# Graph attention and relational message passing: VectorE masks scores ahead of query and output-weight remainders, and half of the last pair's first value row goes in front of the first scores

## The reference, cut to what matters

```python
y = cond_layer_norm(x, cond, ...)
q = (y @ wq + bq).reshape(N, 4, 128) * 128 ** -0.5
k = (y @ wk + bk).reshape(N, 4, 128)
v = (y @ wv + bv).reshape(N, 4, 128)
scores = einsum('ehd,ehd->eh', q[src], k[dst])         # one for each edge and head
attn = softmax of scores over the edges of one source node
x = x + segment_sum(attn * v[dst], src) @ wo + bo
y = cond_layer_norm(x, cond, ...)
x = x + relu(y @ m_w1 + m_b1) @ m_w2 + m_b2
```

## Time and profile before

| | |
|---|---|
| median of three runs | 2318.28 us |
| profiled execution | 2313.26 us |
| its span | 2311.5 us |
| TensorE matmul busy | 2195.7 us, 95% |
| VectorE busy | 1577.9 us, 68% |
| ScalarE busy | 1121.3 us, 49% |
| GpSimd busy | 533.8 us, 23% |

### The profile page before, as it was taken

One profiled execution on the slowest core, in us unless ns is written; L12 is line 12 of the kernel. 1 busy time (PEld: TensorE's weight loads), 2 busy tenths in 40 slices (PEclk: granted clock), 3 DMA queues, 4 the chain that ended last, 5 costly groups with the idle time before them and its releaser, 6 DMA issues.

```text
span 2311.5 us, 36692 instructions
## 1 busy us (share of the span) xinstructions
PE 2195.7 (95%) x13898; PEld 1903.4 (82%) x13898; DVE 1577.9 (68%) x3347; ACT 1121.3 (49%) x1808; POOL 533.8 (23%) x399
## 2 busy tenths in 40 slices
PE   3899979999999999999999999999999999999998
PEld 1565678899888889988888998888899888877877
DVE  9999985588775468877547788754778774343233
ACT  6166643577633357763336775333777533231321
POOL 4000000366400046630005662000665200000000
PEclk9999989999999999999999999999999999999999
DMA  9997781210131020031002103111110421062044
GB/s 250 298 282 243 233 272 35 56 34 23 51 110 31 20 66 23 23 96 68 29 23 63 34 12 109 64 29 31 45 45 1 136 74 29 1 127 37 1 71 106
DMA packets 137379, 189.59 MB, mean 82 GB/s; under 512 B 61285, under 2 KB 61733, under 8 KB 137211
## 3 DMA queue, kind: packets, MB, share of 16 engines
q1 hardware_dynamic: 133208, 180.48, 28.1%
q10 hardware_dynamic: 4003, 6.79, 1.0%
HBM read 155.16 MB, written 32.07 MB: 81 GB/s over the span
## 4 chain that ended last, share of the span: by engine, by line
PE 76%; DVE 12%; ACT 5%; issue 5%; DVEq 1%; DMA 1%; SPq 1%; POOL 0%; ACTq 0%
PE PS L1038 10%; PE PS L1066 9%; PE PS L943 6%; PE PS L945 6%; PE PS L944 6%; PE PS L1052 6%; PE PS L929 5%; PE PS L933 4%; PE PS L930 4%; PE PS L1194 4%; PE PS L1204 4%; PE PS L850 4%; PE PS L801 2%; ACT prob L1435 1%; PE PS L862 1%
## 5 line engine op out<-in xcount | busy, mean ns | idle before, releaser
L782 POOL TENSOR_SCALAR prob<-prob,inv_den 125x1000 f32<-125x1000 f32 x160 | 444.4, 2777 | 0.0
L770 POOL TENSOR_TENSOR rstd<-var_eps,neg_half 125x2 f32<-125x2 f32 x45 | 35.5, 788 | 953.4 <-DVE var_eps L1598 953.4
L1435 ACT ACTIVATE prob<-prob,neg_max 125x1254 f32<-125x1254 f32 x160 | 215.6, 1347 | 56.7 <-DVE neg_max L1950 56.6
L1945 DVE CUSTOM_DVE_ANT_0 prob<-PS,sbias 125x1254 f32<-125x1254 f32 x160 | 233.1, 1457 | 10.0 <-issue 7.3
L1066 PE MATMUL PS<-pT_hi,v_hi 125*128 125x250 f32 x800 | 236.2, 295 | 0.0
L1964 DVE TENSOR_TENSOR pT_lo<-PS,pT_hi 125x1000 fp32r<-125x1000 f32 x160 | 191.1, 1194 | 50.7 <-ACT pT_hi L1452 50.7
L1066 PE MATMUL PS<-pT_lo,v_hi 125*128 125x250 f32 x800 | 224.2, 280 | 0.0
L1066 PE MATMUL PS<-pT_hi,v_lo 125*128 125x250 f32 x800 | 222.6, 278 | 0.0
L1052 PE MATMUL PS<-ident,prob 125*125 125x125 f32 x1600 | 201.1, 273 | 5.6 <-DVE pT_lo L1967 5.5
L1052 PEld LDWEIGHTS PS<-ident,prob 125*125 125x125 f32 x1600 | 195.6, 188 | 12.5 <-issue 7.6
L1450 ACT ACTIVATE pT_hi<-PS 125x1000 fp32r<-125x1000 f32 x160 | 161.9, 1012 | 81.3 <-PE PS L1052 81.3
(11 more groups left out here) (335 smaller groups left out, 5585.6 us busy)
## 6 DMA issues: line engine op xcount, KB each, us to landing
basis_t<-in_L_gnn_basis_dram SPq DMA_DIRECT2D x320, 192.0 KB, 4.9
sbias<-score_bias SPq DMA_DIRECT2D x40, 548.6 KB
adj<-adj SPq DMA_DIRECT2D x20, 546.9 KB
w_lo_raw<-in_L_gnn_m_w_dram SPq DMA_DIRECT2D x8, 1024.0 KB, 6.5
score_bias<-biases SPq DMA_DIRECT2D x10, 548.6 KB
adj<-count SPq DMA_DIRECT2D x10, 546.9 KB
xc<-x_lat SPq DMA_DIRECT2D x12, 448.0 KB
x_first<-x_lat SPq DMA_DIRECT2D x10, 448.0 KB
```

Source lines behind the costliest of these rows:

```text
L782: pool.tensor_scalar(prob[u % 3][:, 0:SPLIT], prob[u % 3][:, 0:SPLIT], inv_den[0:T, u % 4:u % 4 + 1], None, ALU.mult)\
L1435: act.activation(prob[u % 3][:], prob[u % 3][:], ACT.Exp, bias=neg_max[0:T, u % 4:u % 4 + 1], accum_out=den[0:T, u % 4:u % 4 + 1]).then_in ...
L1945: v.tensor_tensor_reduce(prob[u % 3][:].rearrange("p (j s) -> p j s", j=3), PS[0:T, 0:3, 0:SB], sbias[p % 2][a][:].rearrange("p (j s) -> p ...
```

## The change

VectorE's order in attention: for a = 1, q_low(i+1) comes directly behind masking(i, 1); before it stood at the end of a = 0, ahead of masking(i, 1). The first three quarters of the output weights' remainder come in heads 17, 18 and 19, for a = 0, behind pT_low and ahead of the inverse; before they stood at the end of heads 16, 17 and 18. The last quarter comes after head 19 in both. TensorE's order: of the value row (4, 0), 6 matmuls go ahead of scores(0, 0), the 7 others stay behind it. Nothing is added to or taken from what is computed.

```diff
-            def rows(bank, a, x_hi, x_lo, w_hi, w_lo, row3, before=None):
+            def rows(bank, a, x_hi, x_lo, w_hi, w_lo, row3, before=None, chunks=range(4)):
 
                 o = PS[0:T, bank, :]
                 n = slice(T * a, T * (a + 1))
-                for k in range(4):
+                for k in chunks:
                     if before:
                         before(k)
                     pe.matmul(o, x_hi[:, k, n], w_hi[:, k, :], start=(k == 0), stop=False)
...
+                def last_value_rows(a, chunks, row3):
+                    p = NP - 1
+                    return rows(qkv_bank(v_lo_done, 2 * p + a), a, yT_hi[p % 2], yT_lo[p % 2], wv_hi, wv_lo,
+                                row3, chunks=chunks)
+
                 for i in range(4 * NP):
                     for a in range(2):
+                        if i == a == 0:
+                            qkv_bank_free(pe, v_lo_done, 2 * (NP - 1), lay)
+                            last_value_rows(0, (0, 1), None)
                         scores(i, a)
-                        if i == 0:
+                        if i == 0 and a == 0:
+                            last_value_rows(0, (2, 3), bv3).then_inc(v_ps.sem, 1)
+                        elif i == 0:
                             value_rows(NP - 1, a)
                         if i >= 1:
                             turn(i - 1, a)
...
+                def wo_low(k):
+                    wait(v, w_hi_done, lay, k)
+                    v.tensor_tensor(wo_lo[:, k, :], wo_raw[:, k, :], wo_hi[:, k, :].bitcast(fp32),
+                                    ALU.subtract).then_inc(w_lo_done.sem, 1)
+
                 for i in range(4 * NP):
                     for a in range(2):
                         masking(i, a)
+                        if a == 1 and 2 <= i + 1 < 4 * NP:
+                            q_low(i + 1)
                         if i == 0:
                             value_low(NP - 1, a)
                         if i >= 1:
                             pT_low(i - 1, a)
+                        if a == 0 and i > 4 * NP - 4:
+                            wo_low(i - (4 * NP - 4) - 1)
                         inverse(i, a)
-                        if a == 0 and 2 <= i + 1 < 4 * NP:
-                            q_low(i + 1)
-                    if i >= 4 * NP - 4:
-                        k = i - (4 * NP - 4)
-                        wait(v, w_hi_done, lay, k)
-                        v.tensor_tensor(wo_lo[:, k, :], wo_raw[:, k, :], wo_hi[:, k, :].bitcast(fp32),
-                                        ALU.subtract).then_inc(w_lo_done.sem, 1)
+                wo_low(3)
```

## The result

The changed kernel took 2281.0 us, the median of four runs (2279.12 to 2284.91); the kernel before took 2317.93 beside it (four runs, 2311.95 to 2318.28). The ratio is 0.9849, with a 95% interval of 0.9828 to 0.987: faster by 1.5%, some 36 us. The execution profiled took 2284.91 us, its span is 2283.2 us, against 2313.26 and 2311.5 before. Behind TensorE's part the lines stand ten lower, so masking is L1955 (L1945 before), q_low L1879, the inverse L1966 and L1968, pT_low L1974 and L1977, and wo_low has a line of its own, L1982.

A forecast was written before the change was run, and what follows sets the result against it. TensorE was taken as the bound, with its idle time to be won. Terms 1.10 + 0.66 + 2.85 + 2.81 + 0.97 = 8.39 us a layer, 33.6 for four, gave 2279.7 or 2284.6; 2282 was taken, 80% range 2274 to 2297.

The forecast's parts named there:

- The value row: Handover into attention: six value matmuls ahead of the first scores let the second scores come earlier, 1.10 us a layer.
- Both bounds: Value row: 1.40 us of matmuls just fits ahead of the first scores; an open accumulation costs -0.1 to +0.1, taken as 0.
- The head from 1 to 2: Head 1: q_low behind masking lets head 2's first scores start at about 840.72 instead of 841.38, 0.66 us.
- its two bounds: Length of q_low in its new place: between 0.37 and 0.73 us.
- The repeating heads: 15 heads from head 2 to 17: the wait on masking and q_low goes, 0.19 us each, 2.85 us a layer.
- The floor of 9.15: Shortest repeating head if TensorE never stops: 4.56 plus 4.60 us, about 9.15 against the measured 9.334.
- Heads 17 and 18: wo_low behind pT_low lets masking start with its scores; heads fall from 10.65 to 9.20 and 9.29 us, gain 2.81.
- head 19: Last head: second scores come 4.65 us after the first instead of 5.55, carrying 0.97 us into the layer's end.
- The slower rival: q_low is held until GpSimd's normalisation ends, making heads 9.72 us and the kernel 2327 us; chance 0.05.
- q_low as the last release: q_low replaces masking as TensorE's last release, so the repeating heads gain nothing: 2296 us on the median's scale; chance 0.15.
- The margin: Repeating head: q_low releases TensorE 0.15 to 0.2 us before TensorE is ready for the next scores.
- The profile's scale: The profiled execution's 2313.3 us less 33.6 gives 2279.7; the same share off the median gives 2284.6.

The follow-up runs named there:

- e8_nine_ahead: The changed kernel with nine of the 13 value matmuls ahead of the first scores instead of six: 2280.48 us, ratio 0.9854 to the kernel before.
- e1_value: The kernel before with half of the value row ahead of the first scores as the only edit: 2317.82 us, ratio 1.0001.
- e7_before_q_twice: The kernel before with each q_low from head 2 on computed twice in its old place: 2351.97 us, ratio 1.015.
- e5_q_twice: The changed kernel with each q_low from head 2 on computed twice: 2282.83 us, ratio 0.9851 to the kernel before.
- e11_value_filled: The kernel before with the value row edit alone, plus nine unread matmuls in TensorE's wait before head 2's first scores: 2310.5 us, ratio 0.9977.
- e3_outw: The kernel before with the three output-weight remainders moved behind pT_low as the only edit: 2310.93 us, ratio 0.9983.
- e9_q_behind_pT: The changed kernel with q_low one place later, behind pT_low: 2418.84 us, ratio 1.0438 to the kernel before.
- e6_q_thrice: The changed kernel with each q_low from head 2 on computed three times: 2317.48 us, ratio 1.0006 to the kernel before.
- e10_tail: The changed kernel with the last two output-weight quarters' remainders in head 19 and the output bias split earlier: 2279.16 us, ratio 0.9844 to the kernel before.

## Why the prediction was right

It said 2282 us, 2274 to 2297, faster with 0.92; it is 2281.0. What decided is that idle time was read off start-to-start distances and not off wait lists: one of the two largest terms, 2.60 of 8.51 us a layer, was one that no list names. That the total is only 1 us off is in part luck: 2282 was put between 2279.7 on the profile's scale and 2284.6 on the median's, the attention stages gave 34.3 us and the medians differ by 36.9. By its own steps:

- **The value row, 1.10 us a layer.** 1.15. Both bounds held: the cover was just long enough (the first scores 1.95 after the last query columns in both), and an accumulation left open cost nothing seen. `e8_nine_ahead` shows the edge of the cover. What the step missed is the company: alone the edit gives nothing (`e1_value`), and nothing in the prediction said so. Its sum went by terms that were taken as independent, and they were so only because the query edit was in it too.
- **The head from 1 to 2, 0.66.** 1.04. The order of events was right, the size of q_low was not: the prediction took the upper of its two bounds, 0.73, and it took 0.41. The transposes of that head then wait for pT_low (0.15 in the record, at 833.96; they start 0.89 us after the last three scores, where 0.57 is usual). That makes head 2 0.31 us longer than before, so of the 1.04 only 0.73 is left one head later, near the 0.66. The wait did not go, it moved by a head; the prediction asked for scores only.
- **The repeating heads, 15 x 0.19 = 2.85.** 14 x 0.186 = 2.60, for head 2 does not repeat. The floor of 9.15 was 9.149. It was worked out from the half that ran without a stop and from the slow start, 0.82 against 0.74, and `e7_before_q_twice` against `e5_q_twice` shows the loop itself: 0.45 a head for the same instruction in the old order, 0.01 in the new. S0(2) to S0(17) was to be 137.2 and is 137.72; the difference is head 2, 9.63 where 9.15 was reckoned.
- **Heads 17 and 18, 2.81, and head 19, 0.97.** 3.08 and 0.95. The heads were to be 9.2 and 9.29, and are 9.12 and 9.11: TensorE was to wait for q_low until 9.20, with q_low at 0.73; at 0.41 it waits for nothing. `e5_q_twice`, where VectorE spends 0.44 more there, has 9.30 and 9.37, so there is less room here than in heads 3 to 16.
- **The slower rival** (q_low held until GpSimd is done, 2327 us) did not come. The Trainium skill, page "SBUF — State Buffer", section "Who interferes with whom", has the later instruction blocked until the first ends; this trace disagrees: 0.41 us at 1.79 into a pass of 2.78, 0.74 at 0.62 into it. **q_low as the last release** did not come either, but the mechanism is there: at three q_lows TensorE waits for it in each of 18 heads and the gain is gone. The margin was some 0.5 us a head, not the 0.15 to 0.2 that was reckoned, again for the 0.73: 0.32 less for q_low makes 0.47 to 0.52 of it.
- **The two errors of the sum offset each other**: 0.41 instead of 0.73 gave 0.38 in head 1 and 0.27 in heads 17 and 18; head 2 took back 0.50 against its share (0.19 hoped for, -0.31 measured). 8.39 was predicted, 8.51 measured.
- **The profile's scale.** 2279.7 was said for the profiled execution, which took 2284.91. The attention gave what it was to give (34.3 against 33.6); 5.9 us were lost in the first and last stages, where the granted clock was lower (0.96 against 0.97 over the first stage, and the stretches above), which no run ties to the change.

## What to carry to other kernels

Read a loop that repeats without jitter by the distance from start to start, and compare its slowest half with its fastest: a bound engine that stops for 0.1 us a turn appears in no list of waits, and begins again slower by another 0.08. On an engine that serves several consumers in order, put first what the bound engine needs next and behind it what is needed one step later, and ask how many tenths of a microsecond are left until the next one is late: here one place earlier cost 0.19 us a head and one place later 1.8. And when an edit is tried alone, look at the granted clock around it before calling it worthless: a good edit may only show once the stop next to it is gone.

## What the runs showed that was not expected

- The clock falls on short stops in an otherwise busy stage: after waits of 1.05 and 1.94 us, some 5 us apart, the granted clock was 0.66 over the next 5 us, and head 2 took 10.8 to 10.9 us instead of 9.32. With 0.23 instead of 1.94 it never fell (`e11_value_filled`). It is not certain: the same waits in the same order kept the clock in one of the four layers of `e3_outw` and in all four in the profile of before. Over all profiles, the clock fell at the wait ahead of head 2 or right behind it in 8 of 8 layers with waits of 2.39 us and more (`e7_before_q_twice`, `e9_q_behind_pT`), in 8 of 16 with 1.79 to 1.94 (`before`, `e1_value`, `e3_outw`, `e6_q_thrice`), and in none of 32 with 1.34 and less. What decides in the middle group was not found.
- Two equal VectorE subtractions, back to back, both inside one pass of GpSimd, took 0.74 and 0.42 us. The delay is one of the pass's early part, and the traces narrow it further. The q_low at 0.62 us into the pass is late by 0.32, the CAST of `e10_tail` at 0.33 by 0.61, so both behave as if held until 0.94 us into it (an estimate, from these durations against 0.42 for each undisturbed). And the wo_low of the kernel before, 1.1 us into a pass, takes 0.69, where in the changed kernel it takes 0.68 outside one.
- Nearly 6 us between the profiled executions of the two kernels lie in stages that are the same in both, with a different granted clock. Two profiled executions of the changed kernel itself (2283.2 and 2279.0 us) differ there by 4.
